# Attention, routing and experts on one core: the first stage in one block of program, paced loads, and a group's scatters spread over the next block

## The reference, cut to what matters

```python
# x: (2, 2048, 256) f32; 16 heads of 16; E = 8 experts of 256 -> 1024 -> 256, top 2
qkv = x @ qkv_w + qkv_b                      # per head q, k, v of 16 each
q, k = rot(q), rot(k)                        # cos, sin by head index
attn = softmax(q k^T / 4)                    # over 2048 keys, no mask
x = layernorm(x + (attn v) @ out_w + out_b)
n = layer_norm(x, g1, be1)
x2 = x + n + (n @ mix_w + mix_b)
n = layer_norm(x2, g2, be2)
topw, topi = top_k(softmax(n @ router_w), 2)
y = sum over the 2 of topw * (silu(n @ w1[e] + b1[e]) @ w2[e] + b2[e])
out = layernorm(x + x2 + y)
```

## Time and profile before

| what | value |
|---|---|
| median of 3 runs | 1771.72 us (1770.25 to 1776.55) |
| the profiled execution | 1769.97 us |
| its span | 1768.3 us |
| PE busy | 1646.8 us (93%) |
| ACT busy | 1234.6 us (70%) |
| DVE busy | 534.5 us (30%) |
| POOL busy | 491.3 us (28%) |
| mean granted clock of PE | 0.966 |

### The profile page before, as it was taken

The page is one execution under the profiler, slowest core; times in us unless marked ns, Lnnn a source line. Parts: engine busy times, 40 slices in busy tenths (PEclk is TensorE's granted clock), DMA queues, the critical chain, the costliest instruction groups (busy, mean ns, idle before and its releaser), DMA issues.

```text
span 1768.3 us, 46251 instructions
## 1 busy us (share of the span) xinstructions
PE 1646.8 (93%) x17948; PEld 934.9 (53%) x17949; DVE 534.5 (30%) x1421; ACT 1234.6 (70%) x1851; POOL 491.3 (28%) x512
## 2 busy tenths in 40 slices
PE   5986999998999999999999999998999999999991
PEld 3642333333333333333333333337899999999991
DVE  3441122633623623623623624634420000000004
ACT  2436899998997997997997997993344444444441
POOL 4750000121121121121121121123445444444441
PEclk9997999999999998999999999999999999999996
DMA  3567410011101153321101101165567766666645
GB/s 114 191 160 110 76 29 23 23 38 42 40 24 38 46 89 74 79 68 38 36 28 38 36 27 39 36 224 177 157 174 215 202 186 190 186 178 178 178 126 198
DMA packets 108822, 181.69 MB, mean 103 GB/s; under 512 B 14041, under 2 KB 80665, under 8 KB 108473
## 3 DMA queue, kind: packets, MB, share of 16 engines
q1 hardware_dynamic: 95346, 161.40, 31.4%
q0 software_dynamic: 13296, 17.77, 5.7%
HBM read 134.59 MB, written 40.18 MB: 99 GB/s over the span
## 4 chain that ended last, share of the span: by engine, by line
PE 77%; issue 4%; ACT 4%; another core or an unknown queue 3%; DVE 1%; DMA 1%; POOL 0%; SPq 0%; POOLq 0%; ACTq 0%; DVEq 0%
PE at_s L1241 23%; PE at_po L1253 22%; PE at_s L1364 14%; PE at_s L1377 13%; ACT place L1154 4%; PE at_small L1269 3%; PE at_small L1262 1%; PE at_po L1353 1%; DMA rows_out<-place,at_v 1%; DVE cb_ln_stats L578 1%; DVE place L1593 0%; POOL place L1097 0%; DMA place<-rows_out 0%; POOL place L1102 0%
## 5 line engine op out<-in xcount | busy, mean ns | idle before, releaser
L1154 ACT ACTIVATE place<-at_s 128x1024 f32<-128x1024 f32 x1024 | 957.9, 1142 | 92.3 <-PE at_s L1241 51.7
L1241 PE MATMUL at_s<-place 99*32 99x512 bf16 x8192 | 590.5, 388 | 35.1 <-ACT place L1154 24.9
L1253 PE MATMUL at_po<-place,at_v 128*32 128x512 f32 x4096 | 555.5, 602 | 9.4 <-issue 9.1
L1241 PEld LDWEIGHTS at_s<-place 99*32 99x32 bf16 x8192 | 202.7, 96 | 518.0 <-issue 250.2
L1364 PEld LDWEIGHTS at_s<-place 128*128 128x128 f32 x2272 | 265.7, 193 | 4.2 <-issue 0.8
L1364 PE MATMUL at_s<-place 128*128 128x128 f32 x2272 | 266.7, 276 | 0.0
L1171 ACT ACTIVATE place<-at_s,b_turned 128x128 f32<-128x128 f32 x568 | 161.8, 368 | 141.4 <-PE at_s L1364 139.5
L1377 PE MATMUL at_s<-place 128*128 x1136 | 256.9, 379 | 0.4 <-issue 0.4
L1377 PEld LDWEIGHTS at_s<-place 128*128 128x128 f32 x1136 | 210.4, 190 | 26.4 <-issue 0.7
L1253 PEld LDWEIGHTS at_po<-place,at_v 128*32 128x32 f32 x4096 | 132.6, 112 | 121.3 <-issue 23.1
L1016 POOL COPY at_v<-place 128x1024 f32<-128x1024 f32 x32 | 33.2, 1041 | 442.3 <-PE at_po L1253 431.7
(11 more groups left out here) (201 smaller groups left out, 971.7 us busy)
## 6 DMA issues: line engine op xcount, KB each, us to landing
place<-in_w SPq DMA_DIRECT2D x79, 1024.0 KB, 9.1
place<-k_parts SPq DMA_DIRECT2D x48, 256.0 KB, 9.3
place<-q_parts SPq DMA_DIRECT2D x192, 64.0 KB
at_v<-rows_in SPq DMA_DIRECT2D x71, 129.0 KB
x_in<-in_x SPq DMA_DIRECT2D x9, 512.0 KB, 4.8
q_parts<-qk_lower SPq DMA_DIRECT2D x16, 256.0 KB, 2.3
k_parts<-qk_lower SPq DMA_DIRECT2D x16, 256.0 KB, 2.5
at_heads_T<-at_o SPq DMA_DIRECT2D x128, 32.0 KB, 1.9
```

The lines of the kernel that those rows point to most:

```text
L1154: nc.scalar.activation(probs[:, slot(n), :], p_s[n % BUFFERS][:, :], ACT.Exp).then_inc(exp_done, 1)
L1241: last = nc.tensor.matmul(p_s[n % BUFFERS][j:j + 32, s * 512:(s + 1) * 512], k_rows[0:ROWS_M, quad(q).start + h, kt * P + j:kt * P + j + 3 ...
L1253: last = nc.tensor.matmul(p_o[32 * h:32 * h + 32, :], v_one[q % 2][:, h, kt, :], probs[:, slot(q * NG + g), s * 512:(s + 1) * 512], start= ...
```

## The change

What it does:

- `constants`, `project` and `bounds` become one block. Loads are issued in another order (trig, weights, x of group 0, bias, x of group 1, then b1); x of groups 0 and 1 is turned and V of group 0 made before the weights are rotated; the query scale is applied to the trig table. The loops are written out for each group. The norms of a group (`take_norms`: 4 products with a mask of 128x128) follow in the next group's order, the means and bounds of sequence 0 come in groups 5 and 6. V of groups 4 to 7 is made after the last group's q and k, around the bounds of sequence 1. ACT squares k, POOL squares q. The ones rows of K (an instruction of POOL before) are ACT's. The middle and low parts have two buffers.
- The K rows of unit 0 are loaded in groups 5 to 7, the queries of unit 0 at group 7.
- In block 0 the loads of K and queries of units 2 and 3 wait for rounds of unit 0 and for `o_normed`, and the six row vectors are sent one by one, every 4 slots. In block 4 the six K loads of a unit are sent 4 slots apart.
- The eight scatters of group i-2 are sent in block i at given rounds; group 6 goes two by two after tiles 0 to 3, group 7 after tiles 15 to 18 as before.
- One exponential of one column on ACT ahead of block 0.

The core of the diff:

```diff
@@ first stage, order on PE
+                pe.wait_ge(identity_ready, 2)
+                turn_x(0)
+                turn_x(1)
+                pe.wait_ge(wv_ready, 1)
+                take_v(0)
                 pe.wait_ge(weights_rotated, 1)
...
+                for g in range(GROUPS):
+                    if g == 0:
+                        pe.wait_ge(bias_ready, 1)
+                    take_qk(g, 0)
+                    take_qk(g, 1)
+                    if g:
+                        take_norms(g - 1)
+                    take_qk(g, 2)
+                    take_qk(g, 3)
+                    if g + 2 < GROUPS:
+                        turn_x(g + 2)
+                    if g == QC + 1:
+                        average(0)
+                    if g + 1 < V_EARLY:
+                        take_v(g + 1)
+                pe.wait_ge(mean_read, 1)
+                take_v(V_EARLY)
+                take_norms(GROUPS - 1)
+                take_v(V_EARLY + 1)
+                average(1)
+                take_v(V_EARLY + 2)
...
+                nc.tensor.matmul(p_qk[1][:, 0:1], ones[:, :], narrow[:, :], start=True, stop=True).then_inc(counted, 1)
+                take_v(V_EARLY + 3)
@@ loads of block 0 on SP
-                for q in range(1, UNITS):
-                    load_k(sp, dram, keep, 0, q)
...
+                load_first_k(1)
+                load_q(0, 0, 1, 1)
+                sp.wait_ge(scored, 2 * NG + NG // 2)
+                load_first_k(2)
+                load_q(0, 0, 2, 2)
+                repack(0)
+                load_first_k(3)
+                load_q(0, 0, 3, 3)
...
+                repack(1)
+                for k, name in enumerate(rows):
+                    sp.wait_ge(scored, 2 * NG + 2 * NG + (k + 3) * (NG // 8))
                     sp.dma_start(rows[name][:, :], dram[name].partition_broadcast(P)).then_inc(loaded_w, 16)
@@ K of the second sequence
-                    load_k(sp, dram, keep, 1, q)
                     load_q(1, 0, q, QC * UNITS + q)
+                    for n in range(len(K_ORDER)):
+                        sp.wait_ge(scored, 2 * NG + (QC - 1) * NB + (q + 1) * NG + n * (NG // 8))
+                        load_k(sp, dram, keep, 1, q, (n,))
@@ scatters on POOL
+        SEND_ROUNDS = {0: (3, 5, 8, 10, 13, 15), 1: (18, 21)}
...
+                def send_beside(i, rounds, first):
+
+                    for k, at_round in enumerate(rounds):
+                        pool.wait_ge(weighed, (i + 2) * NR + at_round + LEAD)
+                        send(i, first + k)
...
+                        if i >= 2 and q in SEND_ROUNDS:
+                            send_beside(i - 2, SEND_ROUNDS[q], 0 if q == 0 else len(SEND_ROUNDS[0]))
+                        if i >= 2 and q == 1:
+                            end_sending(i - 2)
                         route(i - 1, q)
...
+                        for group, first in ((LAST - 1, 0), (LAST, SEND_AFTER)):
+                            if first <= i < first + GT:
+                                send(group, 2 * (i - first))
+                                send(group, 2 * (i - first) + 1)
+                            if i == first + GT:
+                                end_sending(group)
```

More of the change, by code:

```diff
@@ L76, in constants @@
         lines = E * F // P
[L77 to L118, removed]
+        slot_words = 2 * S
+        room = keep["w1_place"]
         raw = m.sb("qkv_raw", [P, KC + 1, H * 3 * HD], F32)
         trig = m.sb("trig", [P, 2, H, HD // 2], F32)
+        trig_q = m.sb("trig_q", [P, 2, H, HD // 2], F32)
         rot_a = m.sb("rot_a", [P, KC + 1, H, HD // 2], F32)
@@ L212, in _ @@
[L212 to L218, removed]
@@ new lines, in take_v @@
+                def take_v(g):
+                    for kc in range(KC):
+                        pe.wait_ge(xT_ready[kc], g + 1)
+                    for i in range(2):
+                        if g:
+                            pe.wait_ge(v_ready, 2 * (g - 1) + i + 1)
+                        for a in range(2):
+                            tok = (2 * i + a) * P
+                            for kc in range(KC):
+                                last = nc.tensor.matmul(p_v[i][:, a, :], xT[:, g % XT, kc, tok:tok + P],
+                                                        w_v[:, kc, :], start=(kc == 0), stop=(kc == KC - 1))
+                        last.then_inc(v_done, 1)
@@ new lines, in take_qk @@
+                def take_qk(g, ft):
+                    if g:
+                        pe.wait_ge(rest_ready, 4 * (g - 1) + ft + 1)
+                    for kc in range(KC):
+                        pe.wait_ge(xT_ready[kc], g + 1)
+                    for kc in range(KC):
+                        last = nc.tensor.matmul(p_qk[ft][:, :], w_qk[:, kc, ft, :], xT[:, g % XT, kc, :],
+                                                start=(kc == 0), stop=(kc == KC - 1))
+                    last.then_inc(qk_done, 1)
@@ new lines, in take_norms @@
+                def take_norms(g):
+                    turns = min(g + 3, GROUPS)
+                    for kc in range(KC):
+                        pe.wait_ge(xT_ready[kc], turns)
+                    if g:
+                        pe.wait_ge(norms_read, 2 * g)
+                    pe.wait_ge(q_squared, 2 * g + 2)
+                    pe.wait_ge(k_squared, 2 * g + 2)
+                    for out, first in ((p_x[0], 2), (p_x[1], 0)):
+                        for kc in range(KC):
+                            last = nc.tensor.matmul(out[:, :], select[:, kc, :, :].rearrange("p r h -> p (r h)"),
+                                                    squares[:, g % 2, first + kc, :],
+                                                    start=(kc == 0), stop=(kc == KC - 1))
+                    last.then_inc(normed, 1)
@@ new lines, in average @@
+                def average(b):
+                    pe.wait_ge(mean_ready, b + 1)
+                    if b == 0:
+                        pe.wait_ge(v_ready, 2 * V_EARLY - 1)
+                    else:
+                        pe.wait_ge(rest_ready, 4 * GROUPS)
+                    for kc in range(KC):
+                        for c in range(QC):
+                            last = nc.tensor.matmul(p_mean[b][32 * c:32 * c + 32, :], key_mean[:, b, kc, :],
+                                                    hi_all[:, kc, tokens(b * QC + c)],
+                                                    start=(kc == 0), stop=(kc == KC - 1))
+                    last.then_inc(averaged, 1)
```

647 lines of the change are left out of this document (350 added, 297 removed).

## The result

The changed kernel takes 1684.84 us (median of 4, 1683.7 to 1686.84), the kernel before 1771.99 beside it: a ratio of 0.9506 [0.9486, 0.9526]. The prediction was 1693.5. The span of the profiled execution went from 1768.3 to 1683.3 us, by 85.0.

What follows compares the result with a forecast made beforehand. PE was taken as the bound, its chain holding 77% of the span, with time to win at block ends, first stage and block 0. Terms -50.9 - 1.5 + 4 - 23.8 - 6 = -78.2 gave 1693.5 us, range 1676 to 1722.

Steps and rivals of the forecast that it cites:

- Scatters, -50.9: Ends of attention blocks 1 to 7: spreading each group's eight scatters regains all 50.9 us lost to stops and slow clock.
- Only eight did: Scatters: three indirect transfers in a row cost PE nothing in the expert stage; only eight in a row stopped it.
- The rival that the stop follows the scatters: Attention blocks: eight scatters still cost 4.9 us per group when spread, though the clock stays up; 1728 us, chance 0.10.
- that of the block's end alone: Block ends: the unnamed stop belongs there, not to the scatters, so their new places do nothing; 1742 us, chance 0.03.
- Slow clock at the expert stage's start, -1.5: Start of the expert stage: the slow clock also goes, saving an estimated 1.5 us (0 to 3.4).
- DVE beside scatters, +4: Second units of blocks 2 to 7: scatters stretch DVE's normalising and delay PE 0.7 us per block, +4 us (0 to 10).
- it would be +13: DVE in attention: the cost if every scatter held up one whole 1.38 us scaling, instead of the +4 taken.
- First stage, -23.8: Before block 0: the merged projection and bounds stage brings the first score at 122.6 instead of 146.4 us.
- hand-overs: End of the first stage: 3 us (0 to 12) allowed on top of PE's 95.1 us of work.
- The rival of a first stage that does not shrink: First stage: groups 4 to 7 stay at 11.2 us through ACT or stores; 1713 us, chance 0.12.
- Paced loads, -6: Block 0: pacing its loads regains 6 of the 9.7 us lost there (0 to 9.7).
- The second batch's K loads were never a cost.: K loads of the second sequence: they cost nothing before, so the paced-loads term counted no gain from them.

Runs made afterwards that it cites:

- condition H: Runs beside which the kernel before, with an unchanged program, took 1772 us; the changed kernel took 1684.84 us beside one.
- condition L: Runs beside which the kernel before, with an unchanged program, took 1713 us; the changed kernel took 1686.38 us beside one.
- burst_double: Changed kernel with each group's eight scatters sent twice in one go at the block's end, sixteen in all: 1803.74 us, ratio 1.0177, in condition H.
- scatters_alone: Kernel before with spread scatters as its only edit: 1711.43 us, ratio 0.9987, in condition L.
- burst_mid: Changed kernel with all eight scatters in one go in round 8 of the next block's first unit: 1683.59 us, ratio 0.9823, in condition L.
- the experiment: Changed kernel with the first block's loads issued in one run, without the new waits: 1688.85 us, ratio 0.9869, in condition L.
- before_again: Kernel before, unchanged, profiled again: 1713.01 us, ratio 0.9994, in condition L.
- stage_alone: New first stage alone: changed kernel with scatters in one go at block ends and both sets of loads ordered as before: 1692.28 us, ratio 0.9877, condition L.
- k1_paced_2: Repeat of the changed kernel with the second sequence's K loads really spread: 1678.56 us, ratio 0.9469, in condition H.

## Why the prediction was right, and where it was not

The forecast of 1693.5 us was 8.7 too high; its range and its sign held. The predicted sum is -78.2, that of the spans -85.0, so 6.8 of the 8.7 lie in the terms; the rest is how the medians stand to the profiled executions. Term by term, in condition H, where the kernel was profiled:

- **Scatters, -50.9.** Right in condition H, and a little small: a clean block is 124.1 us, not 124.7. The seven blocks give 46.5, and the 8.6 lost in blocks 3 and 4 stand beside it, against 0.7 before: -54.4. The kernel before gives the same by itself: its blocks 1 to 7 take 923.75 us in H and 1146.30 - 277.02 = 869.28 in L. "Only eight did" holds: six spread scatters leave the first unit at 32.16 us (32.12 with none), and the pairs in the expert stage leave that stage at 567.7 us (567.9 before). burst_double shows that the row is the cause, with sixteen. One reading was loose: the unnamed piece that begins at 530.98 lies between two exponentials of ACT. The fifth scatter had been issued by then, not the fourth, and PE went on, slowed, until 535.02. What the prediction could not see is that the term is 0 in condition L: scatters_alone is 0.9987 there, and the whole change is worth 0.9843 instead of 0.9506. The rival that the stop follows the scatters has fallen, and so has that of the block's end alone: it is still there, without a stop. Whether a row of eight in the middle of a unit stops PE in condition H was not run (burst_mid ran in L), nor were spread scatters as the only edit. The scatters are 3.3 us apart at the closest, where 3.7 was foreseen.
- **Slow clock at the expert stage's start, -1.5.** Measured -0.2.
- **DVE beside scatters, +4.** Measured 0. The first norm's last step starts 283.51 - 270.51 = 13.00 us into the second unit of block 1, which has no scatters, and 407.66 - 394.65 = 13.01 in block 2, which has. The rule of the Trainium skill weighed in the prediction (SBUF — State Buffer, Who interferes with whom), by which it would be +13, does not show here, but little of it was put to the test. The scatter of round 18 (398.80, 0.98 us long) begins in the reciprocal, which takes 3.35 us as everywhere, and ends 0.2 us into the multiplication of two SBUF tiles at 399.56, which takes 0.69 as without a scatter. That of round 21 (403.97, 0.96 us) lies beside steps of 0.16 us, and the scalings at 404.99 begin when it is over. So what failed is the step that the scatters of rounds 18 and 21 stretch DVE by 0.65 us each: they meet none of the scalings.

The two rows of DVE in the changed kernel, block 1 and block 2:

```profile
...
283.51 1.23 DVE L1613 TENSOR_TENSOR rt_norm<-rt_norm,rt_be 128x1024 f32<-128x1024 f32 x1
...
407.66 1.23 DVE L1613 TENSOR_TENSOR rt_norm<-rt_norm,rt_be 128x1024 f32<-128x1024 f32 x1
```

- **First stage, -23.8.** The mechanism was right, the size wrong by 7.6: -31.4 measured. The first product starts at 18.48, not 21.5 (3.0 of it, and inside the 17.5 to 23.8 given); from there to the end of PE's work it is 93.2 us, not 95.1 and 3 of hand-overs (4.9); the barrier is 3.3 for 3. No hand-over shows as a term of its own. The rival of a first stage that does not shrink has fallen.
- **Paced loads, -6.** The trace gives -6.8 for block 0, the experiment 2.5 to 6.4. The rule of the Trainium skill that crossing a page of instructions is mostly hidden (Runtime: NRT & Kernel Launch, Instruction fetch mechanics) is not borne out beside filled DMA engines: stops of 4.18 and 3.14 us, each with a packet of instructions in flight. That these stops are the fetch is an inference from the packets, not from a run that changes the program alone.
- **"The second batch's K loads were never a cost."** This step failed. In the kernel before it held within 1 us (before_again, where no other stop covers it); in the changed kernel the same bytes cost 8.6. PE's program stands elsewhere when they run, q and K leave in one go, and the waits that seem to pace them have passed; how the 8.6 us divide between place and density is open. I took a cost that was small at one alignment for one that does not exist, and did not compare the counts in the new waits with that of load_q.

So the error is small because errors stand against each other: 3.5 + 4 + 7.6 + 0.8 = 15.9 us too little foreseen in four terms, against 7.9 of K loads and 1.3 of slow clock too much: 6.7. That they nearly cancel is luck. So is the condition: the sum with the scatters in it fits condition H, in which both kernels of the first pair ran; in L the same change gives 26.9 us and not 78.

## What to carry to other kernels

Spread indirect scatters over work that is long enough; here it cost nothing, and it takes away a stop that some runs have and others do not, so time both kernels side by side more than once before a gain or a loss is believed. When a wait is put in to pace a load, compare its count with that of the waits ahead of it in the same queue: a wait that has passed paces nothing. A stop on "issue" beside filled DMA engines may be instruction fetch that meets the loads: look whether a packet of instructions came late. Here such stops moved with edits of the program and of the loads' places, so judge such loads by what they could meet, not by what they met.

## What the runs showed of the hardware that was not expected

- The stop behind a row of indirect scatters exists in condition H and not in L, with the same program and the same POOL timing: 7.8 us per row of eight in H (54.4 / 7), 0 in L. Chip number 11 was seen in both. What makes the condition is open.
- In H it grows with the number, and more than twice as much for twice as many: the last unit is longer by 5.4 us for eight in one go and by 16.8 for sixteen, and a row costs 7.8 and 16.4 us in all (992.35 us for blocks 1 to 7 of burst_double, 877.24 in the changed kernel). PE, ACT and DVE all stand still while the DMA engines are 29% busy. What they wait for, no record names.
- With the K loads in one run the same 6 MB cost between 1 us (the kernel before) and some 10 (stage_alone); spread over 7 us each they cost 2.1 (k1_paced_2, blocks 3 and 4: 737.69 - 487.32 = 250.4). That instruction fetch is what stretches rests on the late packet ahead of each of the three stops, on the missing late ones where there is no stop, and on the effect of spreading; a run that moves PE's program alone was not made.
